# Key stacks of 128 rows with zeros, returned in two halves, one buffer for both normalised blocks, a second residual load and a new step order in a gated attention layer

## The reference, cut to what matters

```python
x = x + tanh(g_xattn) * xattn(layernorm(x), ctx, ctx, ...)   # 8 heads of 128; cosine, covariance and variance scores, mixed
x = x + tanh(g_ffn) * ffn(layernorm(x), Wq, Wk, Wv, Wo, Wff)

def ffn(x, Wq, Wk, Wv, Wo, Wff):               # 16 heads of 16 features
    q, k, v = split_heads(x @ Wq), split_heads(x @ Wk), split_heads(x @ Wv)
    attn = softmax(einsum('bqd,bkd->bkq', q, k) / sqrt(D), axis=-1)
    z = merge_heads(einsum('bkq,bkv->bqv', attn, v)) @ Wo
    z = l2_normalize(l2_normalize(z) @ Wff)
    return gelu(z)
```

## Time and profile before

| what | value |
|---|---|
| median of 3 runs | 1545.77 us (1540.12 to 1548.11) |
| profiled execution, its own time | 1551.81 us |
| its span, first to last instruction | 1550.1 us |
| mean granted TensorE clock | 0.959 |
| PE, DVE, ACT, POOL busy share | 89%, 79%, 66%, 29% |
| turns 2 to 15, the loop | about 270 to 1410 us of the trace |

### The profile page before, as it was taken

One profiled execution on the slowest core, in us unless ns is written; L12 is line 12 of the kernel. 1 busy time (PEld: TensorE's weight loads), 2 busy tenths in 40 slices (PEclk: granted clock), 3 DMA queues, 4 the chain that ended last, 5 costly groups with the idle time before them and its releaser, 6 DMA issues.

```text
span 1550.1 us, 35088 instructions
## 1 busy us (share of the span) xinstructions
PE 1377.8 (89%) x10624; PEld 817.0 (53%) x10624; DVE 1224.7 (79%) x3180; ACT 1027.7 (66%) x3326; POOL 443.8 (29%) x279
## 2 busy tenths in 40 slices
PE   5888488799999999999999999999999999999855
PEld 2655355455555555555565645555555555555422
DVE  5878656687979888888798888887888889797844
ACT  5564213575767676767677676777776768676766
POOL 1441241314141323233232424141414141414100
PEclk9999599899999999999999999999999999999966
DMA  8420103417070707070716243343535261717060
GB/s 255 142 87 17 31 22 70 72 49 107 16 138 16 138 16 138 16 133 21 111 43 93 61 74 80 60 78 67 86 61 94 51 103 43 111 25 117 15 95 15
DMA packets 125733, 115.12 MB, mean 74 GB/s; under 512 B 8024, under 2 KB 123376, under 8 KB 125680
## 3 DMA queue, kind: packets, MB, share of 16 engines
q1 hardware_dynamic: 125696, 114.66, 38.4%
HBM read 78.40 MB, written 25.32 MB: 67 GB/s over the span
## 4 chain that ended last, share of the span: by engine, by line
PE 30%; DVE 26%; issue 13%; ACT 7%; DMA 6%; SPq 3%; DVEq 1%; POOL 0%; PEldq 0%; ACTq 0%; POOLq 0%; PEld 0%
PE work L749 8%; PE work L751 7%; PE work L750 7%; DVE nm L1428 7%; DMA qstack<-parts 5%; ACT prob L1237 5%; PE score L1154 3%; SPq L1042 3%; PE attended L1166 2%; PE work L1073 2%; DVE vsp L1442 2%; DVE mixed L1386 2%; DVE zz L1408 1%; DVE l2s L1401 1%; DMA parts<-kl 1%
## 5 line engine op out<-in xcount | busy, mean ns | idle before, releaser
L1237 ACT ACTIVATE prob<-score,nm 128x256 f32<-128x256 f32 x1024 | 474.5, 480 | 117.2 <-DVE nm L1428 112.6
L1428 DVE TENSOR_REDUCE nm<-score 128x2 f32<-128x512 f32 x512 | 336.1, 682 | 32.0 <-PE score L1154 31.2
L1154 PE MATMUL score<-qstack,kstack 64*128 64x256 f16 x1024 | 184.2, 281 | 42.1 <-DMA qstack<-parts 22.9
L1237 ACT ACTIVATION_READ_ACCUMULATOR prob<-score,nm 128x1 f32 x1024 | 216.4, 211 | 0.0
L1362 DVE BATCH_NORM_STATS2 qst<-work 128x6 f32<-128x128 f32 x512 | 111.1, 284 | 72.0 <-PE work L751 70.8
L1166 PE MATMUL attended<-prob,vsp 128*32 128x256 f32 x2048 | 143.4, 399 | 22.4 <-DVE vsp L1442 22.4
L1154 PEld LDWEIGHTS score<-qstack,kstack 64*128 64x128 f16 x1024 | 59.2, 96 | 175.3 <-ACT prob L1237 90.7
L1301 POOL TENSOR_TENSOR mixed<-mixed,tmp 128x616 f32<-128x616 f32 x64 | 96.0, 1501 | 177.4 <-DVE mixed L1386 173.7
L1281 POOL TENSOR_TENSOR rq<-qft,mhalf 128x32 f32<-128x32 f32 x16 | 87.0, 5439 | 144.8 <-DVEq L1369 144.8
L1288 POOL TENSOR_TENSOR kTl<-khat,kTh 128x462 f16<-128x462 f32 (+1 forms) x48 | 46.3, 966 | 253.8 <-ACT kTh L1195 253.8
L749 PE MATMUL work<-woutTh,fvph 128*128 128x256 f16 x384 | 107.3, 279 | 0.0
(11 more groups left out here) (291 smaller groups left out, 3573.7 us busy)
## 6 DMA issues: line engine op xcount, KB each, us to landing
krows<-kstat SPq DMA_DIRECT2D x32, 616.0 KB, 5.8
kstack<-parts SPq DMA_DIRECT2D x128, 128.0 KB, 7.8
qstack<-parts SPq DMA_DIRECT2D x128, 128.0 KB, 8.3
s_xin<-in_x SPq DMA_DIRECT2D x8, 1024.0 KB, 6.0
xin<-in_x SPq DMA_DIRECT2D x16, 512.0 KB, 7.4
x<-x2S SPq DMA_DIRECT2D x16, 512.0 KB, 5.3
out<-zb SPq DMA_DIRECT2D x16, 512.0 KB, 4.9
parts<-qh SPq DMA_DIRECT2D x16, 256.0 KB, 2.2
```

Source lines behind the costliest of these rows:

```text
L1154: last = nc.tensor.matmul(sc[n % SC][:, jj * NQ:(jj + 1) * NQ], stack["k"][64 * e:64 * e + 64, j, b2 * NQ + k * P:b2 * NQ + (k + 1) * P], ...
L1237: nc.scalar.activation(prob[:, g % PG, k, u % 4, :], sc[n % SC][:, jj * NQ:(jj + 1) * NQ], ACT.Exp, bias=nm[:, u:u + 1], accum_out=sums[:, ...
L1428: nc.vector.tensor_reduce(nm[:, 2 * n:2 * n + 2], sc[n % SC][:, :].rearrange("p (u q) -> p u q", q=NQ), AX.X, ALU.max, negate=True).then_i ...
```

## The change

- `kstack` gets two planes, one for each half e of the heads. Plane e holds that half's 64 rows; the other 64 partitions are zero, filled once by POOL at the start of the main phase, and SP waits for this fill (`init` at 4) before its first step. The score matmul reads all 128 partitions of plane e and of `qstack`.
- The return is two steps, back0 and back1: columns 0 to 255 and 256 to 511 of both stacks, 16 transfers of 64 KB each, in packets of 512 B, with a semaphore each. back0 waits for the stores and for the first 16 scores of the pair before, back1 for all of them. S0 waits for the first half, S16 for the second.
- `z` and `zz` are one buffer, `norm`. z waits for zz0 and zz1 of the turn before, ln2 for zT0 and zT1 of this turn.
- `xb` goes: a new SP step ldy loads the residual rows from x into `x2S`, POOL adds the bias in place, and y0, y1 add PE's result in place.
- The list ORDER is new.

```diff
 ORDER = """
-xb G0 G0.h G1 G2 G1.h G0.l G2.h G1.l G3 ldr G2.l G4 qs1 G3.h ldx V0 G4.h S0 V0.h G3.l S1 qpow S2 G4.l G5 M0 V1 G5.h
-V0.l X0 M1 M2 V2 V1.h G5.l S3 V2.h V1.l d0 X1 M3 d1 V2.l X2 S4 qs2 X3 d0.o d2 M4 S5 d1.o X4 d3 M5 x0 S6 X5 V3 M6 d2.o
-X6 d3.o R0 S7 x1 S8 M7 V4 M8 X7 V3.h R1 P0 V4.h V3.l V4.l S9 X8 S10 M9 m0 M10 m1 X9 S11 P1 m0.h m1.h m0.l S12 X10 m1.l
-d4 M11 m2 S13 d4.o X11 d5 M12 m2.h d6 X12 m2.l d5.o S14 M13 V5 x2 M14 X13 d7 d6.o S15 R2 X14 S16 M15 P2 M16 X15 d7.o
-S17 E0 y0 x3 R3 X16 V5.h V5.l M17 X17 ldk m3 y0.o S18 m3.h m4 M18 m5 P3 m4.h L0 m3.l m5.h X18 S19 m4.l S20 m5.l fk0
-M19 M20 S21 z fk0.h y1 E1 X19 L1 X20 fk0.l M21 fk0.k R4 zT0 O0 y1.o zT0.h ln1 X21 S22 fk1 zT0.f O0. M22 S23 lpow O1
-fk1.h M23 X22 fk1.l S24 ln2 X23 P4 O1. fk1.k zz0 zT0.l S25 zz0.h zz1 fk2 zz0.l zz1.h kh0 zT1 zz1.l fk2.h S26 kl0 zT1.h
-pq0 fk2.l fk2.k zT1.f M24 pq1 pq0.h M25 X24 pq0.l pk0 R5 X25 M26 pq1.h zT1.l S27 pk0.h pk1 pq1.l X26 pk0.l S28 M27
-pk1.h P5 X27 pk1.l M28 S29 parts S30 M29 X28 q0 M30 X29 R6 S31 X30 q1 M31 q0.o X31 P6 kh1 R7 back E2 kl1 P7 L2 pv0 E3
-kh2 L3 q1.o O2 pv0.v O3 O2. q2 O3. q3 F1 q2.o pv1 q3.o kl2 F2 q4 pv1.v q5 q4.o F3 q6 q5.o q7 q6.o q7.o F4 out res
+qs1 G0 G0.h G1 G2 G1.h S0 G0.l qpow S1 G2.h S2 G1.l G3 G2.l G4 M0 G3.h V0 G4.h G3.l X0 M1 ldr G4.l ldx G5 V0.h M2 S3
+V1 G5.h V0.l X1 G5.l X2 qs2 S4 M3 d0 V1.h M4 d1 X3 V1.l S5 d0.o X4 d2 M5 ldy S6 R0 X5 S7 d3 d1.o M6 x0 S8 V2 d2.o X6
+M7 P0 d3.o X7 M8 S9 V3 z X8 x1 V2.h M9 S10 V3.h S11 V4 M10 X9 R1 xb V2.l X10 M11 S12 P1 V3.l V4.h X11 M12 S13 m0 V4.l
+X12 m1 M13 S14 d4 m0.h R2 m1.h m0.l S15 E0 P2 m1.l X13 M14 m2 d5 m2.h d4.o X14 m2.l d6 d5.o M15 x2 d7 d6.o X15 V5 d7.o
+S16 V5.h S17 zT0 V5.l S18 M16 zT0.h y0 x3 M17 X16 M18 X17 R3 zT0.f ldk X18 S19 y0.o m3 m4 M19 m3.h m5 S20 m4.h m3.l P3
+m5.h X19 m4.l fk0 m5.l M20 zT0.l S21 fk0.h S22 L0 y1 E1 M21 X20 L1 fk0.l X21 M22 R4 X22 fk0.k S23 y1.o zT1 O0 M23
+zT1.h ln1 zT1.f S24 S25 X23 P4 O0. M24 fk1 lpow M25 X24 ln2 S26 O1 fk1.h X25 fk1.l S27 zz0 O1. fk1.k S28 R5 zz1 zz0.h
+M26 fk2 zz1.h zz0.l kh0 P5 zz1.l fk2.h X26 M27 pq0 M28 X27 zT1.l S29 X28 pq1 fk2.l M29 pq0.h fk2.k S30 X29 pq0.l S31
+pk0 M30 pq1.h M31 X30 pk1 R6 X31 pq1.l P6 pk0.h R7 pk1.h pk0.l P7 kh1 pk1.l E2 L2 q0 parts E3 L3 O2 q0.o O3 O2. q1 O3.
+back0 q2 F1 q1.o q3 q2.o kl0 F2 q4 kl1 q5 q3.o F3 q4.o q6 q5.o q7 q6.o back1 pv0 q7.o kh2 F4 pv1 kl2 pv0.v pv1.v out
+res
 """.split()
...
-    xin, xb, zz = w["xin"], sb("xb", [P, PT, DIM]), sb("zz", [P, PT, DIM])
-    z, xTf = sb("z", [P, PT, DIM]), sb("xTf", [P, PR])
+    xin, xTf = w["xin"], sb("xTf", [P, PR])
+    norm = sb("norm", [P, PT, DIM])
...
-    stack = {a: sb(a + "stack", [P, FH // 2, PR], F16) for a in "qk"}
+    qstack, kstack = sb("qstack", [P, FH // 2, PR], F16), sb("kstack", [P, 2, FH // 2, PR], F16)
...
                     sp_wait(z_ready, a)
-                    sp_wait(xb_ready, a)
                     sp.dma_start(xin[:], x_rows[bass.ds(a * PR, PR), :].rearrange("(t p) d -> p t d", p=P)).then_inc(x_ready, 16)
+                elif step == "ldy":
+
+                    sp_wait(zz_ready, a)
+                    sp_wait(x2_in, a * 16)
+                    sp.dma_start(x2S[:], x_rows[bass.ds(a * PR, PR), :].rearrange("(t p) d -> p t d", p=P)).then_inc(y_in, 16)
...
                     sp_wait_drained(a, "pq0", "pq1", "pk0", "pk1")
-                    sp_wait(stack_in, a * 256 + START)
+                    for landed in stack_in:
+                        sp_wait(landed, a * 256 + START)
                     for n, t in enumerate((qk["q"]["h"], qk["q"]["l"], qk["k"]["h"], qk["k"]["l"])):
                         sp.dma_start(parts[n].rearrange("(t p) n -> p t n", p=P), t[:]).then_inc(parts_stored, 16)
-                elif step == "back":
-
-                    sp_wait(parts_stored, a * 64 + 64)
-                    sp_wait(sc_ready, a * SCORES + START)
+                elif step in ("back0", "back1"):
+
+                    b2 = int(step[-1])
+                    cols = slice(b2 * NQ, (b2 + 1) * NQ)
+                    if b2 == 0:
+                        sp_wait(parts_stored, a * 64 + 64)
+                    sp_wait(sc_ready, a * SCORES - (1 - b2) * SCORES // 2 + SC_CREDIT)
                     for c in range(4):
                         for e in range(2):
-                            for name, n in (("k", 2 + c // 2), ("q", c % 2)):
-                                src = parts[n].rearrange("(q e d) n -> e d q n", e=2, d=FD)[e]
-                                sp.dma_start(stack[name][64 * e + FD * c:64 * e + FD * (c + 1), :, :],
-                                             src).then_inc(stack_in, 16)
+                            rows = slice(64 * e + FD * c, 64 * e + FD * (c + 1))
+                            for dst, n in ((kstack[rows, e, :, cols], 2 + c // 2), (qstack[rows, :, cols], c % 2)):
+                                src = parts[n].rearrange("(q e d) n -> e d q n", e=2, d=FD)[e][:, :, cols]
+                                sp.dma_start(dst, src).then_inc(stack_in[b2], 16)
...
+            sp_wait(init, 4)
             run(sp, a_part, b_part)
...
                 if kind in ("zT", "zz"):
-                    src = z if kind == "zT" else zz
                     pe.wait_ge(z_ready if kind == "zT" else zz_ready, a + 1)
                     for t in range(PT):
-                        last = nc.tensor.transpose(bk[:, t * P:(t + 1) * P], src[:, t, c * P:(c + 1) * P], ident[:])
+                        last = nc.tensor.transpose(bk[:, t * P:(t + 1) * P], norm[:, t, c * P:(c + 1) * P], ident[:])
...
                     (b2, t, e), k = unit(n // 4), n % 4 // 2
-                    if n == 0:
-                        pe.wait_ge(stack_in, b * 256 + 256 + START)
+                    if n % (SCORES // 2) == 0:
+                        pe.wait_ge(stack_in[b2], b * 256 + 256 + START)
 
...
                         last = nc.tensor.matmul(sc[n % SC][:, jj * NQ:(jj + 1) * NQ],
-                                                stack["k"][64 * e:64 * e + 64, j, b2 * NQ + k * P:b2 * NQ + (k + 1) * P],
-                                                stack["q"][64 * e:64 * e + 64, j, b2 * NQ:(b2 + 1) * NQ],
+                                                kstack[:, e, j, b2 * NQ + k * P:b2 * NQ + (k + 1) * P],
+                                                qstack[:, j, b2 * NQ:(b2 + 1) * NQ],
                                                 start=True, stop=True)
                     last.then_inc(sc_ready, 1)
...
             nc.gpsimd.memset(vsp[:], 0.0).then_inc(init, 1)
+            nc.gpsimd.memset(kstack[:], 0.0).then_inc(init, 1)
...
                 if e == "xb":
 
-                    pool.wait_ge(x_ready, a * 16 + 16)
-                    pool.wait_ge(v2_ready, a)
-                    nc.gpsimd.tensor_tensor(xb[:], xin[:], bc(w["tb"][:].unsqueeze(1), [P, PT, DIM]),
+                    pool.wait_ge(y_in, a * 16 + 16)
+                    nc.gpsimd.tensor_tensor(x2S[:], x2S[:], bc(w["tb"][:].unsqueeze(1), [P, PT, DIM]),
                                             ALU.add).then_inc(xb_ready, 1)
...
+                    if not (isinstance(a, int) and a == 0):
+
+                        wait_filled(dve, a - 2, "zz0", "zz1")
                     for t in range(PT):
-                        last = nc.vector.tensor_scalar(z[:, t, :], xin[:, t, :], st4[:, t, 0:1], st4[:, t, 1:2],
+                        last = nc.vector.tensor_scalar(norm[:, t, :], xin[:, t, :], st4[:, t, 0:1], st4[:, t, 1:2],
...
                     wait_filled(dve, a, e)
                     dve.wait_ge(xb_ready, a + 1)
-                    dve.wait_ge(x2_in, a * 16)
                     drain(nc.vector.scalar_tensor_tensor(
                         x2S[:, 2 * c:2 * c + 2, :], bank(e)[:, :].rearrange("p (t o) -> p t o", o=DIM), 1.0 / (FV * MS),
-                        xb[:, 2 * c:2 * c + 2, :], ALU.mult, ALU.add), e)
+                        x2S[:, 2 * c:2 * c + 2, :], ALU.mult, ALU.add), e)
...
                     dve.wait_ge(r2_ready, a + 1)
+
+                    wait_filled(dve, a + 1, "zT0", "zT1")
                     for t in range(PT):
-                        last = nc.vector.tensor_scalar(zz[:, t, :], x2S[:, t, :], l2m[:, t, 0:1], l2r[:, t:t + 1],
+                        last = nc.vector.tensor_scalar(norm[:, t, :], x2S[:, t, :], l2m[:, t, 0:1], l2r[:, t:t + 1],
```

## The result

| what | before | changed |
|---|---|---|
| median of 4 runs each | 1546.74 us (1540.12 to 1548.11) | 1560.06 us (1559.30 to 1564.89) |
| profiled execution, its own time | 1551.81 us | 1560.67 us |
| mean granted TensorE clock | 0.959 | 0.926 |

The ratio, estimated from all these runs, is 1.0097, its 95% interval 1.0071 to 1.0123; the two medians alone give 1.0086. So the kernel is slower by about 0.9%, where 1491 us had been forecast, with 0.85 on faster.

What follows compares the result with a forecast made beforehand. PE was taken to bound the kernel. Key stacks -58.5, give-back +15, halves -18 and start +7 made -54.5 against 1551.8 us, 1497.3; less 6.0 for the runs' median, 1491 us, range 1455 to 1535.

Steps and rivals of the forecast that it cites:

- What bounds it: Loop: PE busy 848.2 of 896 us, so nearly every microsecond of PE's stream is a microsecond of the turn.
- Full-height key stacks: PE's scores: 128-row matmuls remove the switches around 64-row pairs, 3.9 us a turn, -58.5 us over 15 turns.
- the give-back: PE's saving partly lost because DVE is late next: 1 us a turn, +15 us, bounds 0 to 30.
- The stacks in two halves: Return on SP: the first score needs half the bytes, landing in 9.5 us with 3.4 us slack; -18 us.
- the slower rival: Return: packets, not bytes, set the rate; a half takes 17 us, score 0 waits every turn; 1571 us, chance 0.11.
- New order: Waits from the new ORDER list: no net change, 2 us a turn each way, 30 us.
- One normalised buffer: DVE's two new waits, z for zz transposes and the second normalisation for zT1: nothing.
- Residual loaded twice: 512 KB more a turn, 2 us of DMA engine time, and POOL's bias add moved later: nothing.
- Start: Fourth zero fill on POOL, 7.1 us, delays SP's first load: +7 us once.

Runs made afterwards that it cites:

- the pair in which only the hold-up is left: Changed kernel with the return undivided at the first half's place, without and with z moved from behind S9 to after S14: 1664.21 and 1600.39 us.

## Why the prediction was wrong, step by step

- **What bounds it: PE.** Right for the kernel before, and the reason why the stalls cost in full. In the changed kernel the chain runs through SP's queue, the input, z beside POOL, and the exponentials.
- **Full-height key stacks.** Right. In the changed kernel's timeline of PE a score pair starts 0.11 us behind a 256-column matmul, and the next full matmul 0.22 us behind the pair: nothing is left of the 0.195 us.

```profile
945.49 0.27 PE L751 MATMUL work<-woutTh,fvpl 128*128 128x256 f16 x1
945.60 0.38 PE L1166 MATMUL score<-qstack,kstack 128*128 128x256 f16 x2
945.82 0.30 PE L749 MATMUL work<-Gh,xTh 128*128 128x308 f16 x1
```

  The Trainium skill ("TensorEngine Tiling (Array Packing)", Key Properties) had it that a change of tiling mode drains TensorE; the trace agrees. The net gain, -58.5 + 15 = -43.5 us, was measured as 41.7 and 42.3 us in the new order. In the old one it is 16.4 us. So the give-back belongs to an order. It was worked out from the old order's rows and came out right for the new one, which is partly luck, above all in the stalled kernel, where another wait sets the turn.
- **The stacks in two halves.** The sign right: score 0 doesn't wait in the loop, and the waits for stacks fell by 12.4 us where 18 were taken. But it was closer than forecast. A half, taken at 9.5 us, lands 11.2 to 12.3 us after its first issue, in the 12 turns from 511 us on, and score 0 comes 0.1 to 1.1 us behind it, not 3.4; at 12.9 us the slower rival would have decided. The last turn still waits 8.1 us: its score 0 starts 17.1 us after the first store instead of 24.0, but PE has work for only 9 us of that time, where it had 15. What wasn't seen is that the halves carry the new order: 129 us.
- **The step that failed** is the one that gave z's move nothing: "New order" took "no net change", and "One normalised buffer" asked only which buffer z waits for, and wrote "Nothing." The diff takes z from S21 to S9, and that place was held neither against the landing of z's input nor against POOL's work. For the first, the prediction had the time itself: "Behind it on SP stand the output, the residual store, the key rows and the next input, as before the change; their data come 1 to 2 us later than now." The size was right (input 32.4 us after the first store instead of 31.0), and in the kernel before the input landed 29.7 us ahead of z; z moved up by 30.6 us against the stores. For the second, the list itself has z between POOL's x0, x1 and xb. The runs showed 2.1 us of waiting and 5.5 us of hold-up on DVE a turn in place of nothing, 88 us in all by the run with z later, and 64 us by the pair in which only the hold-up is left.
- **New order.** It was given 0, within 30 us either way. It cost 88 us at this one place; without it the same order gives 1471.75 us, inside the range, and 19 us better than the forecast. Where these 19 us come from stays open.
- **The slower rival** had the wrong mechanism (packets) and gave 1571; its side note, that key rows and input would be late for POOL's mixing and z, came nearest to the real one. It was priced at 1 us a turn, and z running beside the mixing wasn't in it.
- **Residual loaded twice.** Not nothing in the old order: the load with the moved bias, the fill and the rest cost 15 us there. Which of them wasn't parted. In the new order it shows as an input that lands in 9.2 us instead of 6.7, with the third load issued 4.5 us before it has landed. That load isn't the only difference: in the turn read the last return lands at 947.6, after the input's issue at 945.27, where before it landed at 852.5, ahead of it. What the load alone is worth wasn't tried.
- **Start.** +7 us was taken, for the late load. The first key product is 8.2 us later, but because DVE's z is held during POOL's fill. Fill and wait moved together bring the first product back by 7.3 us and the time by 5.6; the wait alone gives about 5 us of time, though next to nothing at the first product. Where those 5 us lie, and how much of them is spread of the runs, stays open.

Why does DVE's wait of 2.1 us come with a turn that is 5.9 us too long? Because the wait isn't the main cost. z, late or not, stands beside POOL's mixing and bias add, which adds 5.5 us on DVE. Both lie ten scores into the turn, when PE has only three score banks ahead, so the maxima and exponentials behind them follow late together, and PE stands still for nearly all of it. After the stall it runs at the lower clock for a while: 0.94 in the loop instead of 1.00.

## What to carry to other kernels

When a step moves in a hand-written order, hold the landing time of its data, read from the trace before, against its new place on each engine that works in order, and look at what the other engines do at that place: here 2.1 us of lateness and 5.5 us beside POOL's work became 5.9 us a turn. Put the loads of a queue in the order in which they are needed, before touching anything that computes: one swap gave 77 us. And a saving on one engine's stream is worth only what the spacing of the others lets through, so measure it in the order it will live in.

## What the runs showed of the hardware that was not expected

- z (four instructions on DVE) takes 1.38 us alone, 3.14 to 6.51 us beside POOL's mixing and bias add, and 8.22 us beside POOL's 7.06 us fill: one of the four took 7.09 us, the other three 1.1 together. The rule of the Trainium skill ("SBUF — State Buffer", Who interferes with whom) is that DVE in its two-port mode and POOL exclude each other for whole instructions. The trace agrees: the held instruction is as long as the fill.
- After a stall of PE of 4.1 and 1.7 us 16 attended matmuls take 1.93 instead of 1.07 us, at a granted clock of 0.50. With one such stall in every turn the mean granted clock is 0.94 in the loop.
- 64 KB transfers in 512 B packets into 16 partitions run at 114 GB/s in the mean of 12 turns, against 121 for 128 KB in 1,024 B packets, and the 2 MB take 21.1 us from first issue to last landing instead of 20.0. So the halves with half the packets cost about 6% of the rate. Packet and transfer size changed together and weren't parted.
